# A node-update kernel's prologue: halo loads first, low weights on GpSimd, and another order for VectorE's first two steps

## The reference

```python
h   = jnp.maximum(_layernorm(x), 0.0)
agg = segment_sum(edge_attr, dst, 50000) / jnp.maximum(segment_sum(1, dst, 50000), 1.0)[:, None]
out = x + (relu(concatenate([agg, h], 1) @ W1 + b1) @ W2 + b2)     # W1 320x512, W2 512x256
```

## Time and profile before

| | us |
|---|---|
| median of three runs (range) | 1377.42 (1375.92 to 1379.47) |
| profiled execution, its own time | 1376.72 |
| its span | 1375.1 |
| TensorE busy | 1335.7, 97% |
| VectorE busy | 1195.0, 87% |
| ScalarE busy | 695.8, 51% |
| GpSimd busy | 537.3, 39% |

### The profile page before, as it was taken

The page is one execution under the profiler, slowest core; times in us unless marked ns, Lnnn a source line. Parts: engine busy times, 40 slices in busy tenths (PEclk is TensorE's granted clock), DMA queues, the critical chain, the costliest instruction groups (busy, mean ns, idle before and its releaser), DMA issues.

```text
span 1375.1 us, 29825 instructions
## 1 busy us (share of the span) xinstructions
PE 1335.7 (97%) x7076; PEld 1121.4 (82%) x7076; DVE 1195.0 (87%) x2965; ACT 695.8 (51%) x1281; POOL 537.3 (39%) x710
## 2 busy tenths in 40 slices
PE   2699999999999999999999999999999999999998
PEld 1588888888888888888888888888888888888887
DVE  6598989898898989898988989898989888898986
ACT  2354545555454545455555545454555555454543
POOL 4334343443434343434334343434343343434341
PEclk7999999999999999999999999999999999999999
DMA  3345455554545454545555454545455554545452
GB/s 91 97 114 143 111 138 117 133 126 123 131 118 138 110 146 110 140 115 134 122 128 131 119 134 115 145 107 143 113 136 119 131 129 120 131 118 141 110 127 57
DMA packets 422789, 168.78 MB, mean 123 GB/s; under 512 B 321076, under 2 KB 422390, under 8 KB 422776
## 3 DMA queue, kind: packets, MB, share of 16 engines
q1 hardware_dynamic: 421076, 166.67, 50.1%
q10 hardware_dynamic: 1700, 1.97, 0.6%
HBM read 66.30 MB, written 51.40 MB: 86 GB/s over the span
## 4 chain that ended last, share of the span: by engine, by line
PE 96%; DVE 1%; DMA 1%; SPq 1%; issue 0%; ACT 0%; POOL 0%; DVEq 0%; POOLq 0%
PE P L836 27%; PE P L816 14%; PE P L838 14%; PE P L818 13%; PE P L817 13%; PE P L825 6%; PE P L826 6%; PE PA L805 2%; PE PA L806 2%; DMA dst_w<-in_dst_dram 1%; DVE wb_lo L725 0%; SPq L263 0%; DVE wb_lo L724 0%; ACT HN L533 0%; SPq L286 0%
## 5 line engine op out<-in xcount | busy, mean ns | idle before, releaser
L836 PE MATMUL P<-w_both,H_hi 128*128 128x512 f32 x1568 | 560.0, 398 | 9.7 <-DVE H_lo L673 9.7
L559 ACT ACTIVATE H_hi<-P 128x512 fp32r<-128x512 f32 x392 | 233.7, 597 | 512.2 <-PE P L826 512.2
L838 PE MATMUL P<-w_both,H_lo 128*128 128x256 f32 x1568 | 441.4, 281 | 0.0
L673 DVE SCALAR_TENSOR_TENSOR H_lo<-P,H_hi 128x512 fp32r<-128x512 f32 x392 | 269.2, 687 | 115.5 <-ACT H_hi L559 105.7
L836 PEld LDWEIGHTS P<-w_both,H_hi 128*128 128x128 f32 x1568 | 295.4, 188 | 83.0 <-DVE H_lo L673 11.0
L816 PE MATMUL P<-HT_hi,w_hi 128*128 128x512 f32 x784 | 314.3, 401 | 4.2 <-DVE HT_lo L665 4.2
L818 PE MATMUL P<-HT_hi,w_lo 128*128 128x512 f32 x784 | 308.9, 394 | 0.0
L817 PE MATMUL P<-HT_lo,w_hi 128*128 128x512 f32 x784 | 306.1, 390 | 0.0
L838 PEld LDWEIGHTS P<-w_both,H_lo 128*128 128x128 f32 x1568 | 295.0, 188 | 3.8
L433 POOL TENSOR_TENSOR XB<-X,b_row 128x1024 f32<-128x1024 f32 x98 | 236.6, 2415 | 136.1 <-DVE O L684 136.1
L427 POOL TENSOR_TENSOR E_lo<-ES,E_hi 128x256 fp32r<-128x256 f32 x98 | 73.2, 746 | 410.7 <-ACT E_hi L539 410.7
(11 more groups left out here) (76 smaller groups left out, 1136.4 us busy)
## 6 DMA issues: line engine op xcount, KB each, us to landing
X<-in_x_dram SPq DMA_DIRECT2D x97, 512.0 KB, 3.6
HQ<-HN SPq DMA_DIRECT2D x388, 128.0 KB, 3.1
out_dram<-O SPq DMA_DIRECT2D x97, 512.0 KB, 3.3
ER<-in_edge_attr_dram SPq DMA_DIRECT2D x392, 32.0 KB, 1.8
DT<-table_dram SPq DMA_DIRECT2D x392, 1.0 KB, 1.7
X<-in_x_dram ACTq DMA_DIRECT2D x1, 512.0 KB, 6.3
w_raw<-in_L_gnn_W_dram ACTq DMA_DIRECT2D x4, 128.0 KB, 5.9
w_raw<-in_L_gnn_W_dram ACTq DMA_DIRECT2D x2, 256.0 KB, 7.9
```

What stands on the lines that cost most here:

```text
L559: act.activation(H1_hi[:, m, :], bank(m)[:], ACT.Relu).then_inc(s_1hi, 1)
L673: dve.scalar_tensor_tensor(out=H1_lo[:, m, :], in0=bank(m)[:], scalar=0.0, in1=H1_hi[:, m, :], op0=ALU.max, op1=ALU.subtract).then_inc(s_1 ...
L836: pe.matmul(out_bank(j)[:], H1_hi[:, m, rows], w2_both[:, m, :, :].rearrange("p a d -> p (a d)"), start=(m == 0), stop=False)
L838: last = pe.matmul(out_bank(j)[:, 0:D], H1_lo[:, m, rows], w2_both[:, m, 0, :], start=False, stop=(m == CH - 1))
```

## The change

It touches the prologue and the first two steps; the loop over the other tiles stays as it is.

- SyncE waits for both halos before it loads X of tile 1. ScalarE waits for X of tile 0 before it issues the loads of the edge weights and all that follow (bias, W2, b2), and with them everything else in its queue.
- The sum of the search signals when its last matmul is done; the order check has a semaphore of its own, which only `flag_i` waits for.
- wb_lo moves from VectorE to GpSimd, ahead of `norm(0)`, behind a wait for ScalarE's third high part (b1_hi).
- ScalarE: `layernorm(1)` stands ahead of `means_high(0)`, and `hidden_high(0)` ahead of `edges_high(1)`.
- SyncE: `move(1)` stands ahead of `load_x(2)`.
- VectorE's steps 0 and 1 use `first_step`: all four `hidden_low` chunks first, then (in step 0) `ends(1)` and `onehot(1)`, both transposes and HT_lo of the next tile, the residual, and only then `stat`, `aggregate`, `ends` and `onehot` of tile t+2.

```diff
             sp.dma_start(dst_w[1:EP, 0:HALO], before).then_inc(s_dstw, 16)
+            sp.wait_ge(s_dstw, 32)
             load_x(1, 1)
...
             load_windows(1, 1)
+            move(1, 1)
             load_x(2, 0)
-            move(1, 1)
             load_windows(2, 0)
...
+            pool.wait_ge(s_whi, 3)
+            pool.wait_ge(s_const, 14)
+            pool.tensor_tensor(wb_lo[0:DE, :], wa_raw[0:DE, :], wa_hi[0:DE, :], ALU.subtract).then_inc(s_wblo, 1)
+            pool.wait_ge(s_wblo, 1)
+            pool.tensor_tensor(wb_lo[96:P, :], b1_raw[96:P, :], b1_hi[96:P, :], ALU.subtract).then_inc(s_wblo, 1)
+            pool.wait_ge(s_wblo, 2)
             norm(0, 0)
...
+            act.wait_ge(s_x[0], 16)
             for a in range(2):
                 act.dma_start(wa_raw[a * DE:(a + 1) * DE, :], w1[0:DE, :]).then_inc(s_w[1], 16)
...
             edges_high(0, 0)
+            layernorm(1, 1)
             means_high(0)
-            layernorm(1, 1)
+            hidden_high(0)
             edges_high(1, 1)
             for t in range(2):
-                hidden_high(t)
+                if t:
+                    hidden_high(t)
...
             dve.wait_ge(s_srch, 5)
+            dve.wait_ge(s_fallen, 1)
             dve.scalar_tensor_tensor(out=flag_i[:], in0=longest[:], scalar=float(P - GR), in1=PA[0:1, 0:1],
...
+            def first_step(t, b):
+                for m in range(CH):
+                    hidden_low(t, m)
+                if t == 0:
+                    ends(1, 1)
+                    onehot(1, 1)
+                for c in range(CD):
+                    transpose(t + 1, 1 - b, c)
+                transposed_low(t + 1)
+                residual(t, b, 0)
+                means_low(t + 1)
+                for j in range(1, SUB):
+                    residual(t, b, j)
+                stat(t + 2, b, range(SUB))
+                aggregate(t + 2, b)
+                ends(t + 2, b)
+                onehot(t + 2, b)
...
-            dve.wait_ge(s_whi, 3)
-            dve.tensor_tensor(wb_lo[0:DE, :], wa_raw[0:DE, :], wa_hi[0:DE, :], ALU.subtract).then_inc(s_wblo, 1)
-            dve.tensor_tensor(wb_lo[96:P, :], b1_raw[96:P, :], b1_hi[96:P, :], ALU.subtract).then_inc(s_wblo, 1)
...
-            ends(1, 1)
-            onehot(1, 1)
-            step(0, 0)
-            step(1, 1)
+            first_step(0, 0)
+            first_step(1, 1)
...
-                pe.matmul(found[0:1, 0:KS * TILES], ones_bf[0:EP, :], below[:, g, :], start=(g == 0), stop=(g == GP - 1))
+                last = pe.matmul(found[0:1, 0:KS * TILES], ones_bf[0:EP, :], below[:, g, :], start=(g == 0),
+                                 stop=(g == GP - 1))
+            last.then_inc(s_found, 1)
             pe.wait_ge(s_fall, 1)
-            pe.matmul(PA[0:1, 0:1], ones_f[0:EP, :], fall[:], start=True, stop=True).then_inc(s_found, 1)
+            pe.matmul(PA[0:1, 0:1], ones_f[0:EP, :], fall[:], start=True, stop=True).then_inc(s_fallen, 1)
```

More of the change, by code:

```diff
@@ L204, in build @@
         s_fall = sem("s_fall")
+        s_fallen = sem("s_fallen")
         s_found = sem("s_found")
```

## The result

| | before | after |
|---|---|---|
| median (nine runs each) | 1377.05 us | 1381.83 us |
| range | 1375.4 to 1379.47 | 1380.51 to 1382.74 |
| profiled execution, its own time | 1376.72 | 1380.51 |
| its span | 1375.1 | 1378.8 |

The ratio is 1.0033, with a 95% interval of 1.0023 to 1.0043: 4.8 us slower. That is inside the range forecast (1374 to 1384 us), clear of zero, and just over the 0.3% that separated "no change" from "slower"; the interval reaches to both sides of that line.

A forecast was written before the change was run, and what follows sets the result against it. TensorE, busy 97% of the span, was taken as the bound. Waits +5.1, low clock +1.65 and start -4.6 gave +2.2 us on 1376.72, so 1378.9 us profiled and 1379.6 us median; range 1374 to 1384 us.

The forecast's parts named there:

- no change: Whole kernel: time within 0.3% of before, between 1373.3 and 1381.6 us; chance 0.66.
- The path: First five steps at most: only the moment from which TensorE runs without a gap can move; the loop stays.
- The start: Prologue: halos land sooner, wb_lo goes to GpSimd, layer 1 starts at 25.6 us instead of 30.23; 4.6 us gained.
- The bound for halos without a gain: Prologue: if halos land no sooner, b1_hi stays at 17.8 us and 0.9 us of gain is left.
- The alternation of wb_lo and scans: Prologue: GpSimd's wb_lo and VectorE's scans exclude each other and take turns; norm(0) ends at 20.9 us.
- The 7.3 us wait for H_lo goes and two others come: Steps 1 and 2: TensorE waits for E_lo at edge_means, 7.3 and 6.5 us, because stat stands behind the residual.
- hangs on `stat(2)`: Step 1: E_lo(2) depends on stat(2) by four queues; the argument given against the stall simply going.
- at most 0.2 us late: End of step 0: VectorE's OH, transposes and HT_lo end at most 0.2 us after layer 2.
- the clock: After the two long waits TensorE runs at the low clock: 1.65 us more lost, bounds nothing to 3.3 us.
- The stall simply goes: Rival, steps 0 to 2: waits after the start are 1.0 us instead of 9.7; 1362.4 us; chance 0.08.
- Slower by a late b1_hi: Rival, prologue: edge weights or halos land late, b1_hi at 17.8 us, only 0.9 us gained; 1383.3 us; chance 0.23.
- One stall only: Rival, steps 1 and 2: VectorE catches up in step 1, tile 3 isn't late; 1371.4 us; chance 0.06.

The follow-up runs named there:

- run with onehot apart: Against the kernel with stat early: ends(1), onehot(1) moved ahead of step 0's hidden_low, ends(2), onehot(2) ahead of step 0's last residual block; 1368.05 us.
- a better order: Against the run with onehot apart: in step 1 the fourth hidden_low also moved ahead of ends(3) and the transposes of tile 2; 1366.32 us.
- kernel with stat early: Changed kernel with first_step in step 0 only, and there stat(2) and aggregate(2) moved ahead of the transposes; 1368.03 us.

## Why the prediction was right, and where not

- **The path.** That only the moment counts from which TensorE runs without a gap, and that the loop stays: confirmed: both kernels are 3.69 us apart at step 3 and at the last matmul.
- **The start.** 4.6 us forecast, 4.46 measured, and in part by luck. dst_f forecast at 9.64 us came at 10.59 us (the halos were taken 1 us too early). b1_hi was ready at 15.0 us as forecast, but it was not what GpSimd waited for: GpSimd's own queue, late with the halos, let the first wb_lo start at 15.54 us instead of 15.05. The second scan then ended only 0.2 us late (19.43 against 19.2) and the rest of `norm(0)` took 1.6 instead of 1.7 us, so `norm(0)` ended at 20.98 us where 20.9 was forecast; wb_lo 1.28 forecast, 1.26 measured; layer 1 25.6 and 25.77. The bound for halos without a gain, 0.9 us left, was too low: with `dst_f` at 13.17 us, layer 1 started at 28.34 us, 1.9 us ahead of the kernel before. The alternation of wb_lo and scans was as the rows of before had it. That exclusion is the rule of the Trainium skill (SBUF — State Buffer, "Who interferes with whom"), and the 1.83 us of the second scan agree with it.
- **The 7.3 us wait for H_lo goes and two others come**: forecast 7.3 and 6.5, measured 6.92 and 6.97. The three runs with one, two and four `first_step` have one, two and four such waits, and moving `stat` and `aggregate` alone takes the wait of step 1 from 6.9 to 1.8 us, while the wait at layer 1 grows from 1.2 to 2.9. The 7.3 us came out as 6.92 mostly because TensorE asked for E_lo(2) 4.2 us after the residual began, not 3.7; the chain itself took the 11.0 us forecast. That E_lo(2) "hangs on `stat(2)`" is true of the queues only, as said above.
- **Mis-sized: "at most 0.2 us late"** at the start of step 1's layer 1. It was 1.17 us. The step counted OH as 0.9 us, from a place where GpSimd was not adding; it took 2.98 us. The forecast had the exclusion for operations with two input tensors only; a comparison of one tensor with a scalar per partition met it too. The run with onehot apart shows that the 2 us go with the addition beside it. The same section of the Trainium skill (SBUF — State Buffer, "Who interferes with whom") lists tensor_scalar among the operations that can take the shared ports, and the forecast did not draw on that; by it the comparison waits for the whole addition, and the 2.39 us of the one comparison agree.
- **Mis-sized: the clock.** One more stretch of 1.65 us lost was forecast, two of 1.65 and 2.5 us came against one: +2.5 us instead of +1.65. The bound of 3.3 us had it.
- Together these make the +2.2 us of the forecast the +3.7 us of the profiled run; the smaller misses (0.4 us less and 0.5 us more for the two waits, 0.3 us less for the H_lo, 0.1 us at the start) cancel. "No change" at 0.66 was the wrong side of the line by 0.7 us on the median, and 0.20 was given to the side on which it fell. `onehot` had been taken at its shortest, and that alone could only go up.
- **The rivals.** "The stall simply goes" is what a better order gives: 1366.3 us where it named 1362.4. "Slower by a late b1_hi" did not happen; b1_hi came at 15.0 us. The time fell near that rival's for other reasons, `onehot` and the clock. "One stall only" did not happen either; the run with `first_step` once has one stall, and 1371.85 us where the rival named 1371.4.

## What to carry to other kernels

When an engine's order is changed to unblock one consumer, follow each step that moved back to the engine that uses its result last: here the queues of GpSimd, ScalarE and GpSimd again stand behind VectorE's `stat`, 5 us of work ahead of E_lo that nothing hides once it starts late. Ask also whether the consumer needs the step's result or only stands behind it in a queue: E_lo does not need `stat`. Do the steps with a long tail behind them first, and move back only the one that waits for a DMA. And undo the parts of a change one at a time: `first_step` hid that `stat(2)` now had to wait for X. Where two engines shut each other out, look for what the other one is doing at the new place, not only at the old.

## What was not expected of the hardware

- `onehot`, four VectorE comparisons of 128x128, each of one tensor with a scalar per partition, took 2.98 us beside a GpSimd addition of 2.40 us and 0.87 us without it: 2.98 and 3.02 us at the two places of the kernel with stat early, 0.87 and 0.88 us when both were moved away.
- A GpSimd operation on four elements (`veps`) takes 0.61 to 0.64 us beside a scan, 0.20 alone.
- The low clock after a wait of 7 us lasted 3.31 us once and 5.02 us once in the same execution.
